# Masks first in every second unit of maxima, one cast for queries and keys of the second attention, and another interleaving of the streams

## The reference, cut to what matters

```
q, k = split_heads(x @ Wq.T + bq), split_heads(x @ Wk.T + bk)     # layer 0, from the normed x
q, k = split_heads(x @ Wq.T), split_heads(ctx @ Wk.T)             # layer 1, no bias
scores = where(causal, q @ k.T / sqrt(32), -inf)
x = x + merge(softmax(scores) @ v) @ Wo.T
```

## Time and profile before

| | us |
|---|---|
| median of 3 runs | 1713.17 |
| lowest and highest | 1711.69, 1718.19 |
| the profiled execution, its own time | 1709.06 |
| its span | 1707.2 |
| PE busy | 1407.3 (82%) |
| DVE busy | 1372.5 (80%) |
| ACT busy | 1034.3 (61%) |
| POOL busy | 434.4 (25%) |

### The profile page before, as it was taken

The page is one execution under the profiler, slowest core; times in us unless marked ns, Lnnn a source line. Parts: engine busy times, 40 slices in busy tenths (PEclk is TensorE's granted clock), DMA queues, the critical chain, the costliest instruction groups (busy, mean ns, idle before and its releaser), DMA issues.

```text
span 1707.2 us, 30917 instructions
## 1 busy us (share of the span) xinstructions
PE 1407.3 (82%) x11862; PEld 726.6 (43%) x11920; DVE 1372.5 (80%) x2111; ACT 1034.3 (61%) x1862; POOL 434.4 (25%) x486
## 2 busy tenths in 40 slices
PE   2777878777989898888877867889998999998986
PEld 2344435243444453434333323435454555454542
DVE  6979989998689796895878799977697878877743
ACT  3333274462763755754576769885898796978431
POOL 2522042331240421321240230231131313031310
PEclk9888889799999998998999989879999998998998
DMA  6303221202002012002030003101010101101020
GB/s 230 97 27 86 51 69 50 58 14 43 27 14 70 2 41 43 26 8 51 21 122 26 2 25 111 36 10 41 26 42 26 41 32 36 37 18 41 14 51 25
DMA packets 92081, 76.37 MB, mean 45 GB/s; under 512 B 9377, under 2 KB 73889, under 8 KB 91425
## 3 DMA queue, kind: packets, MB, share of 16 engines
q1 hardware_dynamic: 91936, 74.40, 16.0%
HBM read 39.24 MB, written 9.44 MB: 29 GB/s over the span
## 4 chain that ended last, share of the span: by engine, by line
DVE 34%; PE 33%; ACT 12%; issue 9%; SPq 5%; POOL 3%; DMA 2%; ACTq 0%; DVEq 0%; POOLq 0%
PE bank L194 10%; DVE mix_NM L1035 6%; DVE ssm_HS L1495 4%; PE bank L1135 3%; SPq L704 3%; PE bank L503 2%; PE bank L948 2%; DVE ffn_m L1089 2%; POOL attn_P L687 2%; DVE ffn_Z L1099 2%; PE bank L511 2%; PE bank L491 2%; PE bank L933 2%; ACT ssm_DA L1443 2%; PE bank L463 1%
## 5 line engine op out<-in xcount | busy, mean ns | idle before, releaser
L1008 ACT ACTIVATE mix_P<-bank 128x512 f32<-128x512 f32 x256 | 141.8, 604 | 60.6 <-PE bank L933 59.6
L1035 DVE TENSOR_REDUCE mix_NM<-bank 128x2 f32<-128x512 f32 x256 | 163.7, 683 | 16.5 <-PE bank L908 16.5
L687 POOL TENSOR_SCALAR_AFFINE_SELECT cross_P<-cross_P 128x256 f32<-128x256 f32 x128 | 95.3, 754 | 301.8 <-ACT cross_P L595 301.7
L1495 DVE TENSOR_TENSOR_SCAN ssm_HS<-ssm_DA,ssm_DD 128x1024 f32<-128x1024 f32 x64 | 151.1, 2361 | 20.5 <-ACT ssm_DD L1446 14.7
L687 POOL TENSOR_SCALAR_AFFINE_SELECT attn_P<-attn_P 128x256 f32<-128x256 f32 x128 | 99.9, 791 | 248.1 <-ACT attn_P L595 247.8
L1253 POOL TENSOR_TENSOR ffn_room<-ffn_room 128x512 f32<-128x512 f32 x64 | 87.7, 1370 | 247.3 <-ACT ffn_room L1192 140.5
L1443 ACT ACTIVATE ssm_DA<-ssm_Z,A_T 128x255 f32<-128x255 f32 x256 | 111.7, 500 | 6.8 <-DVE ssm_HS L1495 6.5
L595 ACT ACTIVATE attn_P<-bank 128x384 f32<-128x384 f32 x128 | 63.6, 497 | 56.7 <-PE bank L492 55.9
L595 ACT ACTIVATE cross_P<-bank 128x384 f32<-128x384 f32 x128 | 62.8, 491 | 50.6 <-PE bank L492 50.2
L933 PE MATMUL bank<-mix_Q,mix_K 64*128 64x256 f16 x512 | 53.5, 288 | 37.5 <-DMA mix_Q<-mix_NQL 20.9
L1418 ACT ACTIVATE ssm_Z<-bank 128x512 f32<-128x512 f32 x128 | 72.2, 601 | 19.7 <-PE bank L1331 19.2
(11 more groups left out here) (404 smaller groups left out, 4092.0 us busy)
## 6 DMA issues: line engine op xcount, KB each, us to landing
attn_stack<-attn_P SPq DMA_DIRECT2D x64, 128.0 KB, 2.5
cross_stack<-cross_P SPq DMA_DIRECT2D x64, 128.0 KB, 2.5
ffn_room<-f_gate SPq DMA_DIRECT2D x4, 1024.0 KB, 5.9
XR<-x SPq DMA_DIRECT2D x8, 512.0 KB, 8.1
attn_stack<-attn_P SPq DMA_DIRECT2D x64, 64.0 KB, 2.2
ffn_room<-f_up SPq DMA_DIRECT2D x4, 1024.0 KB, 5.1
ffn_room<-f_down SPq DMA_DIRECT2D x4, 1024.0 KB, 4.8
x_mid<-XR SPq DMA_DIRECT2D x8, 512.0 KB, 3.1
```

The costliest lines, as they stand in the source:

```text
L687: nc.gpsimd.affine_select(out=diagonal, in_=diagonal, compare_op=ALU.is_ge, fill=0.0, base=0, pattern=[[0, 2], [1, P]], channel_multiplier ...
L1008: nc.scalar.activation(self.p[h % 8], bank[b4[h % 2]][:, :], ACT.Exp, scale=HD2 ** -0.5).then_inc(s["p_ready"], 1)
L1035: nc.vector.tensor_reduce(self.nm[:, t, 16 * i + 2 * g:16 * i + 2 * g + 2], bank[b4[u % 3]][:, :].rearrange("p (c k) -> p c k", c=2), AX.X ...
L1495: nc.vector.tensor_tensor_scan(flat(self.hs), flat(self.da), flat(self.dd), 0.0, ALU.mult, ALU.add).then_inc(s["hs_ready"], 1)
```

## The change: what it does

- In units 1, 3, 5, 7, 9 and 11 of both attentions the mask is written first and the scores are added to it. In the four of these units that have 256 columns for a head, each of the two score matmuls of 256 columns becomes two of 128.
- The parts of `qk` have a new order: high queries, low queries, high keys, low keys. In the attention without bias ACT casts queries and keys of a bank in one instruction of 512 columns, and DVE splits them in one.
- By that order the low queries and high keys still lie side by side, but the high queries and low keys don't. One DMA in four becomes two of half the size: a row has 20 DMAs at the place of L704, in both attentions.
- All five strings of turns are new. Each has as many turns of every stream as before.
- The three weight loaders use one set of semaphores, so the second and third wait for the one before them.

```diff
-        Q_LOW, K_HIGH, Q_HIGH, K_LOW = range(4)
+        Q_HIGH, Q_LOW, K_HIGH, K_LOW = range(4)
...
+                if i == 0 and self.before is not None:
+                    sp.wait_ge(*self.before.ready())
...
-                    if u < 4:
-                        for c in range(DC):
-                            nc.tensor.matmul(bank[b][:, c * P:(c + 1) * P], q[:, c, 0:P], k[:, c, 0:P],
-                                             start=(c == 0), stop=False)
-                        last = nc.tensor.matmul(bank[b][:, :].rearrange("p (c k) -> p c k", c=DC), ident16[:],
-                                                broadcast(hide_qk[:, :], 1, DC), start=False, stop=True)
...
+                    masked = u % 2 == 1
+                    for part in ("mask", "scores") if masked else ("scores", "mask"):
...
+                        if part == "mask" and u < 4:
+                            last = nc.tensor.matmul(bank[b][:, :].rearrange("p (c k) -> p c k", c=DC), ident16[:],
+                                                    broadcast(hide_qk[:, :], 1, DC), start=begins, stop=ends)
...
+                                for keys in (slice(0, P), slice(P, S)) if masked else (slice(0, S),):
+                                    last = nc.tensor.matmul(bank[b][:, i * S + keys.start:i * S + keys.stop], q[:, c, P:S],
+                                                            k[:, c, keys], start=(begins and i == 0),
+                                                            stop=(ends and i == 1 and keys.stop == S))
...
-                            pe.wait_ge(self.stack_in, 16 * 16 * (n + 1))
+                            pe.wait_ge(self.stack_in, 16 * 20 * (n + 1))
...
+                    if self.bq is None:
+                        last = nc.scalar.copy(self.qk[:, Q_HIGH:K_LOW:2, c, :],
+                                              bank[self.b[(2 + c) % 3]][:, :].rearrange("p (i k) -> p i k", i=2))
...
+                        last = nc.vector.tensor_tensor(self.qk[:, Q_LOW:K_LOW + 1:2, c, :], src,
+                                                       self.qk[:, Q_HIGH:K_LOW:2, c, :], ALU.subtract)
...
-                                           (2, slice(0, 2), slice(Q_HIGH, K_LOW + 1))):
+                                           (2, slice(0, 1), slice(Q_HIGH, Q_HIGH + 1)),
+                                           (2, slice(1, 2), slice(K_LOW, K_LOW + 1))):
...
 TURNS0 = {
     "sp": (
-        "eacleaaakkkackkebcbeeebbeebccbeeccebccbeccbccbdaccbdaccbccdabccbccdccbccbdccjmmfmfmmmccdfcdfnnnd"
+        "eleaakckkkkbacebeceabebeebccabecceccbebecccbbdacccdccabbccdaccbbccccbcdcbcmdmffcmmjmmccdcfnndnfd"
```

More of the change, by code:

```diff
@@ new lines @@
+        "aaaaaaaaaaaaaaaacaaaaacaaaaaaaaaaaaaaaaaaaaaaaaaaccaaaaacacaaaaaaaaaaaaaaaabaaabbabaaaaaaaaaaaaa"
+        "caaaabacaaaaaabacaaabaabaaaabacaaabbabaabbaaaaaaabaaabaaabaabaaaabaaacbaaaabaaaacaaaaabaaababbbb"
+        "aaaabacabcabbbaaabbaaaabaabbbaabacbbacbbaabbbbbbaaaaaaaaaabbbbabaaabcbbababababbabacbaabaaaabaab"
+        "abaababaaaaabaabbbababaababacbaaacabaabbabbaababbabababcabbbbababbbcaaaaaaaabbbaabccbaabaabaabdd"
+        "bddbabddbabdabdbdabaaadabdabaadbbdaaabaaddbadbaabaaabbdbdadbbddbdadadaadbbadddddababaabbabaddbad"
@@ L243, in __init__ @@
                     self.loaded, self.high_ready, self.low_ready = before.loaded, before.high_ready, before.low_ready
-                self.first = 0 if before is None else len(before.items)
-                self.used = [0 if before is None else len(range(i, len(before.items), len(stage))) for i in range(len(stage))]
+                self.before = before
+                self.first = 0 if before is None else before.first + len(before.items)
+                self.used = [0 if before is None else before.used[i] + len(range(i, len(before.items), len(stage)))
+                             for i in range(len(stage))]
             def ready(self, count=None):
@@ new lines, in pe @@
+                    for part in ("mask", "scores") if masked else ("scores", "mask"):
+                        begins, ends = part == ("mask" if masked else "scores"), part == ("scores" if masked else "mask")
+                        if part == "mask" and u < 4:
+                            last = nc.tensor.matmul(bank[b][:, :].rearrange("p (c k) -> p c k", c=DC), ident16[:],
+                                                    broadcast(hide_qk[:, :], 1, DC), start=begins, stop=ends)
+                        elif part == "mask":
+                            last = nc.tensor.matmul(
+                                bank[b][:, :].rearrange("p (c k) -> p c k", c=2)[:, :, P:S], ident16[:],
+                                broadcast(hide_qk[:, :], 1, 2), start=begins, stop=ends)
+                        elif u < 4:
+                            for c in range(DC):
+                                last = nc.tensor.matmul(bank[b][:, c * P:(c + 1) * P], q[:, c, 0:P], k[:, c, 0:P],
+                                                        start=(begins and c == 0), stop=(ends and c == DC - 1))
+                        else:
+                            for i in range(2):
+                                c = 2 * ((u - 4) // 4) + i
+                                for keys in (slice(0, P), slice(P, S)) if masked else (slice(0, S),):
+                                    last = nc.tensor.matmul(bank[b][:, i * S + keys.start:i * S + keys.stop], q[:, c, P:S],
+                                                            k[:, c, keys], start=(begins and i == 0),
+                                                            stop=(ends and i == 1 and keys.stop == S))
@@ L1777, in build @@
                 (whole(xkv_w), M["xkv"].rearrange("p (a n) -> p a n", a=2))],
-                [z[:, 8 * i:8 * i + 8, :].rearrange("p h t -> p (h t)") for i in range(3)])
+                [z[:, 8 * i:8 * i + 8, :].rearrange("p h t -> p (h t)") for i in range(3)], weights_0)
             weights_f = Loader("l1f", [
```

145 lines of the change are left out of this document (64 added, 81 removed).

## The result

| | us |
|---|---|
| changed kernel, median of 4 runs | 1752.51 (1741.36 to 1756.21) |
| kernel before beside it, median of 4 runs | 1712.43 (1709.83 to 1718.19) |
| ratio of the times, 95% interval | 1.0214, 1.0189 to 1.0239 |
| the profiled execution, its span | 1754.43, 1752.6 |

The change makes the kernel slower by 32 to 41 us. (Of all executions in this document one, of e15, took 5671 us; the ratios leave it out.) I had forecast 1703.8 in 1684 to 1726, and slower with a chance of 0.20. The page of the changed kernel, to be laid beside the earlier trace rows: PE's busy time is 19.9 us less, and the chain's share of SP's queue went from 5% to 11%, that of the stack transfers (L704, now L717) from 3% to 10%.

What follows compares the result with a forecast made beforehand. No single engine was taken as the bound; only time on the chain of waits (DVE 34%, PE 33%) counts. Terms -9.8 + 3.0 + 3.0 + 3.4 - 4 - 1 - 1 - 3 = -9.4 us from 1713.2 gave 1703.8, range 1684 to 1726.

Steps and rivals of the forecast that it cites:

- Four more DMAs a row: SP's queue, all 16 rows: stacks 2.6 us longer delay what is queued behind; +9.4 us in three terms.
- Mixing's maxima ahead of the stack: SP's queue in mixing: maxima DMAs no longer wait behind the stack, which has cover; -9.8 us together.
- Last row: Second attention's last row: longer stack and a store in between delay the maxima and first scores; +3.0 us.
- mixing's keys at 782: First layer's last attention row: mixing's keys wait behind the longer stack and one more store; +3.0 us.
- Masks: PE's mask and score units: paired masks save tiling switches, counted only at the lower clock; -4 us, bounds 0 and -19.
- Casts: ACT and DVE: one 512-column cast replaces a pair, counting only a row's last pair; -1 us, bounds 0 and -6.
- The start: Kernel start: Wv's load lands up to 3.4 us earlier, but DVE is busy; -1 us, between 0 and -3.4.
- The rest of the turns: Other reordered turns: remove more waits than they add, unpriced in the trace; -3 us, bounds -12 and +12.
- the queue decides: Rival: the longer stack and what is queued behind it hold up each row's scores; 1730 us, chance 0.20.
- Given back: Rival: mixing's scores start earlier but find ACT and PE taken, so 9.8 us return; 1713.6 us, chance 0.25.
- PE's freed time counts: Rival: PE's 19 us from masks are not lost waiting for DVE; 15 us more gain, 1689 us, chance 0.13.

Runs made afterwards that it cites:

- e15: Kernel before with new turns, sixteen stack transfers, several first-layer turns moved back, masks first, second attention's maxima directly behind the stack; 1693.87 us, ratio 0.9855.
- e4: Changed kernel with sixteen stack transfers a row again instead of twenty; 1714.0 us, ratio 0.9987 to the kernel before.
- e2: Kernel before with the new parts order, merged casts and twenty stack transfers a row, old turns, masks last; 1743.97 us, ratio 1.0161.
- e7: e2 with sixteen stack transfers a row instead of twenty; 1712.24 us, ratio 0.9986 to the kernel before.
- e8: Kernel before with 24 stack transfers a row instead of 16, same bytes, nothing else; 1789.65 us, ratio 1.0439.
- e13: e9 with the stacks of the first attention's rows 4, 5 and 6 ahead of mixing's maxima on SP's queue; 1712.8 us, ratio 0.9964.
- e5: e1 with the stack of the first attention's row 3 back ahead of mixing row 1's maxima on SP's queue; 1705.75 us, ratio 0.9953.
- e1: Kernel before with only the five new strings of turns and the loaders' semaphores, sixteen stack transfers; 1711.02 us, ratio 0.9961.
- e3: Kernel before with only the masks put first in every second unit; 1702.14 us, ratio 0.9922.
- e9: e5 with the last pair of row 0's low parts moved earlier among DVE's weight-rounding passes; 1700.65 us, ratio 0.9917.
- e6: Kernel before with masks first and new turns only from the second attention's first row on, sixteen transfers, casts apart; 1689.42 us, ratio 0.9854.
- e10: e6 with 8 of a row's 16 stack transfers in the second attention issued from POOL's queue; 1675.57 us, ratio 0.9775.

## Why the prediction was wrong, point by point

- **Four more DMAs a row, +9.4: the step that failed.** The duration was right (0.60 us an issue, 13.6 a stack); the exposure was not. Measured +39 in the new turns, +30 in the old. It failed in two places. For the second attention's rows 0 to 6 I wrote "its bounds are 0 and +13.5" and "I take a quarter", because PE would have other work in the gap. From C0 to C7 the four transfers took 23 us in the changed kernel (after against e4), above the upper bound too, and 9 (e2 against e7) to 20 (against before) in the old turns. For the first layer I charged one row of eight; there it came to 10 us at A7 (after against e4), and 6 (e2 against before) to 11 (against e7) in the old turns. For the second attention the trace of before had the number that says so: how long SP itself waited, once the stack was out, for the split of the maxima (us, times, longest).

```profile
SPq L710 <- DVE cross_NQL L647: 5.3, 4, 1.9
```

5.3 us in all 8 rows is 0.7 a row that could hide an added 2.6. I looked at PE, which took up the scores as soon as the maxima landed, and then trusted that it had other work; the queue had hardly any slack. The same reading says less of the first layer: there 2 to 32 us lay between a stack's end and its maxima, the maxima still went out on time in six of 8 rows in e2 and in five in e8, and time was lost all the same. On which path it was lost there stays open.
- **Mixing's maxima ahead of the stack, -9.8.** Half right. e13 undoes it in rows 4 to 6 and loses 8 us, so there the sign and size hold, and with them the cover costed at nothing. In row 3, of which I spoke only in the rival, e5 makes it a cost of 5 us by the medians, not told from nothing. The wait that was to go is still there: L933, now L946, waits 21.4 us for these transfers, for 20.9 in the earlier trace rows, and in the fifth row they start at 449.66 for 422.09, since all stands later by then; the gap behind the split, which ended at 449.63, is gone as forecast. SP's queue after, for the earlier trace rows:

```profile
449.66 0.51 SPq L893 DMA_DIRECT2D mix_Q<-mix_NQH  x1
...
452.16 13.53 SPq L717 DMA_DIRECT2D attn_stack<-attn_P  x20
...
813.34 14.05 SPq L717 DMA_DIRECT2D attn_stack<-attn_P  x20
827.43 0.59 SPq L879 DMA_DIRECT2D ctx_parts<-mix_CTH  x1
```

- **Last row +3.0, mixing's keys at 782 +3.0.** The terms are of the right size where they can be read: the stack at 813.34 takes 14.05 us for 10.46, from A7 to C0 after takes 3.9 us more than e4, and from C7 to the end 3.6 more. They belong to the 39.
- **Masks, -4.** Under-sized: -9 to -17 alone, within the bounds. DVE does set the pace at the upper clock, as said: the masks stand in pairs 1.2 us apart, 0.60 a unit for 0.54. PE after, in the last row:

```profile
1671.66 0.56 PE L465 MATMUL bank<-hide_qk,ident 128*128 128x256 bf16 x2
...
1672.86 0.67 PE L465 MATMUL bank<-hide_qk,ident 128*128 128x256 bf16 x2
```

In the new turns masks and casts together gave nothing (e4 against e1: +0.0026, intervals overlap); why the gain of e3 vanishes there was not found. PE's busy time did fall, from 1387.7 us in e1 to 1370.8 in e4, but no longer where the chain passes.
- **Casts, -1.** Right within what can be told (e7: 0.9986).
- **The start, -1.** Wrong sign. Wv's load no longer stood in the chain, PE began at 34.13 for 33.86, and the first stack began at 54.48 for 48.86, and undoing one place of DVE's order brings it back to 49.56 (e9), with 5 us less by the medians. I had named the passes that were moved, and followed them to `attn_XL` instead of to the low parts that the stack waits for.
- **The rest of the turns, -3 in ±12.** All turns together are -3 to -11 (e1). That small sum hides +23 in the first layer (e4 against e6) and -12 to -24 in the second attention.
- **The rival "the queue decides", 1730.** It had the sign and the mechanism, and its condition was met: PE idle for over 2 us before the first scores in 14 of 16 rows. The condition is a weak one, since e4 meets it in 10 rows without any loss. It was 22 us short, mostly since it used the same bound of 13.5.
- **The other rivals.** "Given back" and "PE's freed time counts" don't describe the result. e13 shows that mixing's gain is not given back in rows 4 to 6, and e3 that PE's freed time does count in the old turns, 13 us alone where that rival had all 19, but nothing in the new.

The terms don't add up either. Alone, turns (-7), masks (-13) and transfers with casts (+28) give +8; together they are +37. Of the 29 between, 9 are the transfers' higher price in the new turns (33 to 44 for 22 to 38, so itself not certain) and most of the rest the masks' lost gain.

## What to carry to other kernels

Where all transfers are issued from one queue, price an added issue at its full duration (here 0.60 us each, 64 of them 39 us) unless the trace shows that the queue itself waits for what comes next in every row; its own wait is the slack, not the idle time of the engine behind it. Measure, too, how late a transfer goes out behind the instruction that makes its data: between two kernels that differ in issues alone, this shows the queue's part directly. Slack at one transfer is no proof that a row costs nothing, as the first layer shows. Read what is queued between a stage's two sets of transfers: putting stores and loads behind the small transfer that the scores need was worth 16 us here, as much as any change to the engines. Finally, cut a new order in two before judging it, since a small sum can be a gain and a loss of 20 us each.

## What was not expected of the hardware

- An issue of a stack transfer costs 0.60 us of SP's queue at either size: 16 transfers of 64 KB and 128 KB or 24 of 64 KB have the same median (0.610 and 0.601 us). Bytes don't set it for others either: a load of 512 KB took 0.38 us of the queue (L1825), the 8 KB of the maxima 0.57 to 0.59.
- Eight of these transfers issued by POOL took 10.7 us in e10's fifth row, 1.3 us each with gaps of 2 and 4 us counted in, twice SP's price; the issues alone are 0.58. The Trainium skill (DMA: Bandwidth & Descriptors, "Specifications") gives some 1 us for GpSimd's path and 0.6 for SyncE's as the latency to the first byte. These traces show no first bytes; that SP's 0.60 us an issue is the same size may be chance.
- The two transfers of the maxima, 8 KB each, issued 0.6 and 1.2 us behind the last of 1.5 MB of loads, took 5.1 and 6.4 us to land instead of 1.9.
- With the same matmuls, the kernels with more issues on SP's queue were granted a lower clock for PE on average: 0.890 in e8 for 0.918 before, and 0.911 after for 0.921 in e4.
